# Reciprocal roots of both layer norms moved from VectorE's Newton steps to GpSimd's power

## The chip, the core and the metric

The kernel runs on one core of one Trainium2 chip. The metric is the device time of one execution in microseconds; less is better. The core has five engines that run their own instruction queues and wait for each other by semaphores: TensorE (PE), VectorE (DVE), ScalarE (ACT), GpSimd (POOL) and SyncE (SP), which here only issues DMAs.

## The reference

One transformer layer over x of 8 batches, 256 tokens, 256 features, in fp32. Attention has 32 query heads (two sets of 16) over 16 key and value heads of 16 features, with a causal mask and a full softmax. The MLP is a gated one of 1024 features plus a routed one of 128, scaled by a weight from the two largest of 8 router logits. Both halves end in a norm without weights:

```
m = mean(z); v = var(z)                      # over the 256 features
norm(z) = (z - m) / sqrt(v + 1e-5)
x1  = norm(x + (y1 - sigmoid(x Wlam) * y2) Wo)
out = norm(x1 + shared_mlp(x1) + routed_mlp(x1) * comb)
```

y1 and y2 are the attention outputs of the two sets of heads. Tokens lie on partitions in two tiles (t = 0, 1) of 128, so a norm of one batch needs 2 tiles x 128 reciprocal roots: a [128, 2] operand, one or two elements in each partition.

## The kernel before, in words

Matrix products are done as three TensorE products of high and low parts (`product`, L624 to L628). The high part is a ScalarE copy, the low part a subtraction on VectorE or GpSimd.

The batches go through a software pipeline, `iteration(i)` for i = 0 to 7 on every engine, each with its own order of work written out by hand. Iteration i holds: the scores and softmax of batch i; the first norm, the router and the gate and up products of batch i-1; the down products and the second norm of batch i-2; and the q, k, v projections of batch i+1.

The first half of an iteration is the score stage: 22 units (`s_unit`, L684 and L689) in a ring of three PSUM banks. Unit u can start only when VectorE has taken the row maximum (`row_max`, L998) of unit u-3. Between the units TensorE does projections (behind units 3, 6, 10), down products of batch i-2 (behind 1, 5, 8, 12), the transposes of x1 (behind 11), and the router (behind 15). VectorE puts one small piece of the first norm of batch i-1 behind each of its first seven row maxima: `norm_mean`, `norm_half`, `norm_seed`, three times `norm_newton`, and `ln_shift` (L983). ScalarE applies it in `first_norm` (L503), behind `first_part(i + 1, 1)`.

The second half has 8 groups of two heads. For each, TensorE makes transposed scores (L710, L714), ScalarE takes exponentials (`exps`, L473), GpSimd sets the masked ones to zero (`causal`, L384, two instructions a group), TensorE multiplies by v (`pv_group`, L738) two groups later, and VectorE copies the result out (`evacuate_pv`, L1019). Behind the last group TensorE transposes y (L751): the first half when groups 0 to 6 are copied, the second when group 7 is. Three MLP units of batch i-1 lie between the groups, and GpSimd makes the low parts of h (`h_rests`, L374). The second norm of batch i-2 starts on VectorE behind the copy of group 0, has a Newton step behind those of groups 1, 2, 3, and its end (`second_norm_end`, L1106, two instructions) behind that of group 4.

GpSimd's queue in an iteration: low part of the next batch's x (`split_xt`, L353); low parts of its projections (`rest_part` L359, `third_part` L365), which take turns with ScalarE's parts; sums of batch i-2; masks and `h_rests`.

VectorE's reciprocal root: half of (v + eps), a first guess from the bits of the float (shift, then subtract from a constant), and three Newton steps. Each step waits for the one before it by a semaphore (`settle`).

After the loop comes a tail: the first norm of batch 7, the rest of batch 6's MLP and its second norm, the MLP of batch 7 in 9 units (`gu_units`, `mlp_unit`, `h_rests`), and then `last_tile` for both tiles. There VectorE alone does two sums, the statistics, the root and the normalisation of a tile, and SP stores it.

Of the kernel before, what the change touches and what calls it, by code (L numbers as in the profile page):

```python
# [52 lines left out]
NEWTON = 3  # L53
LN_STEPS = 2 * TT + 3 + (TT + 1) * NEWTON
NORM1_STEPS = LN_STEPS + 1
# [32 lines left out]
RSQRT_SEED = float(0x5F3759DF - 0x400000)  # L88
# [4 lines left out]
I32 = mybir.dt.int32  # L93
# [5 lines left out]
def build_layer(nc, x, xT, w_proj, w_out, w_gu, w_down, w_router, out):  # L99
    with ExitStack() as ctx:  # L100
# [46 lines left out]
        ln_i = sb("ln_i", [P, 2, TT], I32)  # L147
# [60 lines left out]
        attn_step = sem("attn_step")  # L208

# [118 lines left out]
        def _(pool):  # L328
# [9 lines left out]
            pool.wait_ge(const_step, STACKS + 4)  # L338
# [16 lines left out]
            def rest_part(b, n):  # L355
                pool.wait_ge(qk_raw_done, (b - 1) * QK_JOBS + n + 1)
                pool.wait_ge(qk_h_done, b * QK_JOBS + n + 1)
                raw = psum_order(rest_slot(b, n))
                pool.tensor_tensor(raw, raw, part_order(0, n), ALU.subtract).then_inc(qk_rest_done, 1)  # L359

# [37 lines left out]
            def iteration(i, has_next, has_prev, has_last):  # L398
                if has_next:
                    split_xt(i + 1)  # L400
                    for n in range(QK_JOBS):
                        rest_part(i + 1, n)
                        third_part(i + 1, n)
# [8 lines left out]
                for g in range(1, GROUPS):  # L412
                    causal(i, range(g, g + 1))
                    if has_prev and g - 1 in FF_SCORES:
                        n = FF_SCORES[g - 1]
                        h_rests(i - 1, range(n, n + 1))
# [10 lines left out]
            h_rests(B - 1, range(FF_UNITS))  # L427
# [3 lines left out]
        def _(act):  # L431
# [66 lines left out]
            def first_norm(b):  # L498

                act.wait_ge(attn_step, (b + 1) * ATTN_STEPS)  # L500
# [426 lines left out]
        def _(dve):  # L927
# [22 lines left out]
            def norm_half(which, step, settle):  # L950
                settle()
                step(dve.tensor_scalar(ln_t[:, which, 0, :], ln_mv[:, which, :, 1], EPS, 0.5, ALU.add, ALU.mult))

            def norm_seed(which, step, settle):

                seed = ln_i[:, which, :]
                settle()
                step(dve.tensor_scalar(seed, ln_t[:, which, 0, :].bitcast(I32), 1, None, ALU.logical_shift_right))
                settle()
                step(dve.tensor_scalar(ln_t[:, which, 1, :].bitcast(I32), seed, -1.0, RSQRT_SEED, ALU.mult, ALU.add))  # L960

            def norm_newton(which, step, settle):

                half_var, r, a = ln_t[:, which, 0, :], ln_t[:, which, 1, :], ln_t[:, which, 2, :]
                settle()
                for t in range(TT):
                    step(dve.scalar_tensor_tensor(a[:, t:t + 1], r[:, t:t + 1], r[:, t:t + 1], half_var[:, t:t + 1], ALU.mult, ALU.mult))
                settle()
                step(dve.scalar_tensor_tensor(r, a, 1.5, r, ALU.subtract, ALU.mult, reverse0=True))

            def first_norm_step(n, step, settle):

                if n == 0:
                    norm_mean(0, step, settle)
                elif n == 1:
                    norm_half(0, step, settle)
                elif n == 2:
                    norm_seed(0, step, settle)
                elif n < NEWTON + 3:
                    norm_newton(0, step, settle)  # L980
                else:
                    settle()
                    step(dve.scalar_tensor_tensor(ln_shift[:, :], ln_mv[:, 0, :, 0], -1.0, ln_t[:, 0, 1, :], ALU.mult, ALU.mult))  # L983

# [110 lines left out]
            def second_norm_start(b, step, settle):  # L1095
# [3 lines left out]
                norm_half(1, step, settle)  # L1099
                norm_seed(1, step, settle)  # L1100

            def second_norm_end(b, step, settle):
                settle()
# [5 lines left out]
            def last_tile(t, step, settle):  # L1109
# [3 lines left out]
                half_var, r, a = ln_t[:, 1, 0, one], ln_t[:, 1, 1, one], ln_t[:, 1, 2, one]  # L1113
# [10 lines left out]
                settle()  # L1124
                step(dve.tensor_scalar(half_var, ln_mv[:, 1, t, 1:2], EPS, 0.5, ALU.add, ALU.mult))  # L1125
                settle()
                step(dve.tensor_scalar(ln_i[:, 1, one], half_var.bitcast(I32), 1, None, ALU.logical_shift_right))  # L1127
                settle()
                step(dve.tensor_scalar(r.bitcast(I32), ln_i[:, 1, one], -1.0, RSQRT_SEED, ALU.mult, ALU.add))  # L1129
                for _ in range(NEWTON):  # L1130
                    settle()
                    step(dve.scalar_tensor_tensor(a, r, r, half_var, ALU.mult, ALU.mult))  # L1132
                    settle()
                    step(dve.scalar_tensor_tensor(r, a, 1.5, r, ALU.subtract, ALU.mult, reverse0=True))  # L1134
                settle()
                dve.tensor_scalar(z, z, ln_mv[:, 1, t, 0:1], r, ALU.subtract, ALU.mult).then_inc(out_done, 1)  # L1136

            def iteration(i, has_prev, has_last):
# [5 lines left out]
                for u in range(S_UNITS):  # L1144
                    row_max(i, u)
                    if has_prev:

                        if u < NEWTON + 4:
                            first_norm_step(u, *before)
# [13 lines left out]
                for g in range(GROUPS):  # L1163
# [96 lines left out]
```

## Time and profile before

| | |
|---|---|
| median of 3 runs | 504.98 us (504.73 to 506.27) |
| profiled execution: its own time | 506.3 us |
| its span, first to last instruction | 504.6 us |
| TensorE busy | 426.5 us, 85% |
| VectorE busy | 329.9 us, 65% |
| ScalarE busy | 238.7 us, 47% |
| GpSimd busy | 226.6 us, 45% |
| mean granted TensorE clock | 0.947 of 2.4 GHz |

A row of a timeline is an instruction (or several alike, xN): start in us from the span's start, duration, engine, line of the kernel, operation, output<-input by the program's names, shapes. In brackets stands how long the engine had been idle before and what ended that. PE is TensorE's matmuls, PEld its weight loads.

### The profile page before, as it was taken

To read this page: it belongs to the slowest core of one execution; us is meant where nothing else is said; L and a number is where in the kernel's file an instruction comes from. 1 tells how busy PE (TensorE), PEld (TensorE's weight loads), DVE (VectorE), ACT (ScalarE), POOL (GpSimd) and SP (SyncE) were. 2 spreads that over 40 slices of the span, in tenths; PEclk is the share of its full clock that TensorE was granted. 3 is DMA by queue.
4 is the path that set the end of the run, shared out by engine and by line. 5 is a ranking of instruction groups with operands and counts; after the bars stand their busy time and mean duration, and the time that the engine had idled before them with its cause. 6 is when DMAs were issued, how large, how long until landed. Compare 5 with 4: busy or idle time off the path is not lost. (4 is left out here: it accounts for less than half of the span.)

```text
span 504.6 us, 10452 instructions
## 1 busy us (share of the span) xinstructions
PE 426.5 (85%) x4008; PEld 340.2 (67%) x4008; DVE 329.9 (65%) x882; ACT 238.7 (47%) x532; POOL 226.6 (45%) x283
## 2 busy tenths in 40 slices
PE   5106596799999999989899999999999998997994
PEld 5105334676688758976698568865887678766984
DVE  3503614873478586886787677857786769776685
ACT  4600384237535672548434843576255831582240
POOL 8200465426526572447334743656254731373041
PEclk9755979879999999999999999999999999999999
DMA  8793498128703690249212950378024910000000
GB/s 299 165 124 49 117 132 173 32 84 115 99 2 99 92 133 27 68 90 136 58 38 83 126 105 11 107 92 121 22 76 74 136 46 0 5 2 22 1 23 21
DMA packets 34371, 40.43 MB, mean 80 GB/s; under 512 B 3856, under 2 KB 27920, under 8 KB 34064
## 3 DMA queue, kind: packets, MB, share of 16 engines
q1 hardware_dynamic: 34320, 39.75, 43.3%
q8 instruction: 32, 0.52, 0.5%
q14 instruction: 19, 0.16, 0.1%
HBM read 27.94 MB, written 11.53 MB: 78 GB/s over the span
## 5 line engine op out<-in xcount | busy, mean ns | idle before, releaser
L998 DVE TENSOR_REDUCE neg_max<-ring 128x2 f32<-128x512 f32 (+3 forms) x176 | 105.8, 635 | 40.2 <-PE ring L689 38.3
L473 ACT ACTIVATE prob<-ring 128x512 f32<-128x512 f32 x192 | 100.7, 612 | 14.7 <-PE ring L710 14.5
L374 POOL TENSOR_TENSOR h_lo<-h_full,h_hi 128x256 fp32r<-128x256 f32 x72 | 53.0, 736 | 108.0 <-ACT h_hi L433 108.0
L384 POOL TENSOR_SCALAR_AFFINE_SELECT prob<-prob 128x512 f32<-128x512 f32 x128 | 83.9, 679 | 32.7 <-ACT prob L473 32.7
L626 PE MATMUL ff<-x1T_hi,wg_lo 128*128 128x256 f32 x288 | 85.7, 298 | 1.2 <-DVE h_full L1014 1.2
L628 PE MATMUL ff<-x1T_hi,wg_hi 128*128 128x256 f32 x288 | 80.3, 279 | 0.0
L627 PE MATMUL ff<-x1T_lo,wg_hi 128*128 128x256 f32 x288 | 80.3, 279 | 0.0
L684 PE MATMUL ring<-mask_b,ident_b 128*128 128x128 bf16 (+2 forms) x176 | 46.0, 262 | 32.4 <-DMA k_stack<-qk_parts_dram 27.2
L481 ACT ACTIVATE gate_t<-ff 128x256 f32<-128x256 f32 x72 | 27.6, 384 | 76.5 <-PE ff L628 73.7
L689 PE MATMUL ring<-k_stack,q_stack 96*128 96x256 bf16 (+3 forms) x512 | 61.2, 241 | 0.0
L738 PE MATMUL ybank<-prob,v_ones 128*32 128x256 f32 (+1 forms) x1024 | 55.7, 335 | 3.3 <-issue 2.0
L626 PEld LDWEIGHTS ff<-x1T_hi,wg_lo 128*128 128x128 f32 x288 | 54.2, 188 | 4.7 <-DVE h_full L1014 3.2
L627 PEld LDWEIGHTS ff<-x1T_lo,wg_hi 128*128 128x128 f32 x288 | 54.3, 188 | 0.0
L1008 DVE SCALAR_TENSOR_TENSOR gate_t<-gate_t,ff 128x256 f32<-128x256 f32 x72 | 30.1, 418 | 36.7 <-ACT gate_t L481 36.0
L628 PEld LDWEIGHTS ff<-x1T_hi,wg_hi 128*128 128x128 f32 x288 | 54.1, 188 | 0.0
L1019 DVE COPY yv<-ybank 128x256 f32<-128x256 f32 x64 | 27.0, 422 | 40.6 <-PE ybank L738 40.6
L359 POOL TENSOR_TENSOR rest<-rest,parts 128x512 f32<-128x512 f32 x21 | 24.4, 1161 | 64.5 <-ACT parts L433 64.4
L710 PE MATMUL ring<-q_stack,k_stack 98*128 98x512 bf16 x128 | 41.4, 396 | 8.0 <-ACT prob L473 4.2
L738 PEld LDWEIGHTS ybank<-prob,v_ones 128*32 128x32 f32 x1024 | 27.4, 109 | 27.8 <-DVE yv L1019 7.5
L684 PEld LDWEIGHTS ring<-mask_b,ident_b 128*128 128x128 bf16 x176 | 17.4, 99 | 40.6 <-issue 27.4
L433 ACT ACTIVATE rest<-ybank 128x512 f32<-128x512 f32 x21 | 12.5, 594 | 67.6 <-PE ybank L628 67.6
L689 PEld LDWEIGHTS ring<-k_stack,q_stack 96*128 96x128 bf16 x512 | 38.0, 103 | 3.6 <-issue 1.1
(166 smaller groups left out, 954.8 us busy)
## 6 DMA issues: line engine op xcount, KB each, us to landing
q_stack<-qk_parts_dram SPq DMA_DIRECT2D x48, 256.0 KB, 9.5
qk_parts_dram<-parts SPq DMA_DIRECT2D x72, 128.0 KB
k_stack<-qk_parts_dram SPq DMA_DIRECT2D x8, 384.0 KB, 14.8
xt_raw<-xT SPq DMA_DIRECT2D x8, 256.0 KB, 2.8
k_stack<-qk_parts_dram SPq DMA_DIRECT2D x8, 256.0 KB, 11.7
xz<-x SPq DMA_DIRECT2D x8, 256.0 KB, 3.6
out<-xz SPq DMA_DIRECT2D x7, 256.0 KB, 2.2
prob<-w_gu SPq DMA_DIRECT2D x1, 1152.0 KB, 7.0
```

Source lines behind the costliest of these rows:

```text
L374: pool.tensor_tensor(h_lo[:, n, :], h_full[:, n % RING, :], h_hi[:, n, :].bitcast(F32), ALU.subtract).then_inc(h_lo_done, 1)
L384: pool.affine_select(out=v, in_=v, compare_op=ALU.is_ge, fill=0.0, base=0, pattern=[[0, 2], [HALF, 2], [0, 2], [1, HALF]], channel_multipl ...
L473: act.activation(prob[:, g % RING, u, :], ring[u][:, :], ACT.Exp, scale=SCALE).then_inc(exp_done, 1)
L626: pe.matmul(o, lhs_lo, rhs_hi, start=first, stop=False)
L627: pe.matmul(o, lhs_hi, rhs_lo, start=False, stop=False)
L628: return pe.matmul(o, lhs_hi, rhs_hi, start=False, stop=last)
L684: pe.matmul(o[:, :, keys - HALF:keys], ident_b[:, :], mask_b[:, :].unsqueeze(1).to_broadcast([P, len(columns), HALF]), start=True, stop=Fa ...
L689: mm = pe.matmul(o[:, j, :], q_stacks[b % STACKS][rows, row, block, i * P:(i + 1) * P], k_stacks[b % STACKS][rows, row, block, 0:keys], st ...
L710: mm = pe.matmul(ring[u][:, :], keys_of(b, rows, n, slice(0, P)), q_pair(b, rows, n, slice(0, 2 * T)), start=True, stop=True)
L738: mm = pe.matmul(bank[V_COLS * j:V_COLS * (j + 1), t * P:T], v_ones[:, t, 2 * g + j // 2, :], p, start=(t == 0), stop=(t == TT - 1))
L998: dve.tensor_reduce(neg_max[:, columns.start:columns.stop, i], ring[u % RING][:, 0:len(columns) * keys].rearrange("p (h k) -> p h k", k=keys),
L1008: dve.scalar_tensor_tensor(gate_t[:, n % RING, :], gate_t[:, n % RING, :], 1.0, ff[n % 2][:, 0:T], ALU.add, ALU.mult).then_inc(gate_done, 1)
```

## The change

All reciprocal roots leave VectorE. GpSimd computes v + eps with a `tensor_scalar` and raises it to the power -0.5 with a `tensor_tensor` against a constant tile `minus_half`, set once at the start. For the first norm it also makes -mean and the product -mean * root (`ln_shift`). VectorE keeps the statistics (`norm_stats`, `norm_mean`) and the normalisation; ScalarE's `first_norm` waits for the new semaphore `norm1_scale`.

In GpSimd's queue the first norm's scale stands behind `split_xt` and ahead of the first `rest_part`; the second norm's behind the mask of group 3. `second_norm_end` on VectorE now stands behind the copy of group 5, not 4. In the tail `first_scale(7)` comes first, `second_scale(6)` behind the low parts of MLP units 0 and 1, `second_norm_end` behind unit 4 as `SCALE_UNIT + 2`, and the last two tiles' scales behind all of h.

```diff
-NEWTON = 3
-LN_STEPS = 2 * TT + 3 + (TT + 1) * NEWTON
-NORM1_STEPS = LN_STEPS + 1
+LN_STEPS = 2 * TT
+NORM1_STEPS = LN_STEPS
+SCALE_STEPS = 4
+SCALE_GROUP, SCALE_UNIT = 3, 2
+LAST_STEPS = 3
...
+            def first_scale(b):
+                base = b * SCALE_STEPS
+                pool.wait_ge(attn_step, (b + 1) * ATTN_STEPS)
+                if not is_first(b):
+                    pool.wait_ge(x1_done, b * TT)
+                pool.tensor_scalar(ln_t[:, 0, 0, :], ln_mv[:, 0, :, 1], 1.0, EPS, ALU.mult, ALU.add).then_inc(norm1_scale, 1)
+                pool.tensor_scalar(ln_t[:, 0, 2, :], ln_mv[:, 0, :, 0], -1.0, 0.0, ALU.mult, ALU.add).then_inc(norm1_scale, 1)
+                pool.wait_ge(norm1_scale, base + 2)
+                pool.tensor_tensor(ln_t[:, 0, 1, :], ln_t[:, 0, 0, :], minus_half[:, :], ALU.pow).then_inc(norm1_scale, 1)
+                pool.wait_ge(norm1_scale, base + 3)
+                pool.tensor_tensor(ln_shift[:, :], ln_t[:, 0, 2, :], ln_t[:, 0, 1, :], ALU.mult).then_inc(norm1_scale, 1)
+
+            def second_scale(b):
+                pool.wait_ge(norm2_step, (b + 1) * LN_STEPS)
+                if not is_first(b):
+                    pool.wait_ge(out_done, b * TT)
+                pool.tensor_scalar(ln_t[:, 1, 0, :], ln_mv[:, 1, :, 1], 1.0, EPS, ALU.mult, ALU.add).then_inc(norm2_scale, 1)
+                pool.wait_ge(norm2_scale, 2 * b + 1)
+                pool.tensor_tensor(ln_t[:, 1, 1, :], ln_t[:, 1, 0, :], minus_half[:, :], ALU.pow).then_inc(norm2_scale, 1)
...
                     split_xt(i + 1)
+                if has_prev:
+                    first_scale(i - 1)
+                if has_next:
                     for n in range(QK_JOBS):
...
                     causal(i, range(g, g + 1))
+                    if has_last and g == SCALE_GROUP:
+                        second_scale(i - 2)
...
-            h_rests(B - 1, range(FF_UNITS))
+            first_scale(B - 1)
+            h_rests(B - 1, range(SCALE_UNIT))
+            second_scale(B - 2)
+            h_rests(B - 1, range(SCALE_UNIT, FF_UNITS))
+            for t in range(TT):
+                one = slice(t, t + 1)
+                pool.wait_ge(last_norm_step, LAST_STEPS * (t + 1))
+                if t == 0:
+                    pool.wait_ge(out_done, (B - 1) * TT)
+                pool.tensor_scalar(ln_t[:, 1, 0, one], ln_mv[:, 1, t, 1:2], 1.0, EPS, ALU.mult, ALU.add).then_inc(last_scale, 1)
+                pool.wait_ge(last_scale, 2 * t + 1)
+                pool.tensor_tensor(ln_t[:, 1, 1, one], ln_t[:, 1, 0, one], minus_half[:, one], ALU.pow).then_inc(last_scale, 1)
...
-                act.wait_ge(attn_step, (b + 1) * ATTN_STEPS)
+                act.wait_ge(norm1_scale, (b + 1) * SCALE_STEPS)
...
-                        if u < NEWTON + 4:
-                            first_norm_step(u, *before)
+                        if u == 0:
+                            norm_mean(0, *before)
...
-                        elif g <= NEWTON:
-                            norm_newton(1, *norm2)
-                        elif g == NEWTON + 1:
-                            second_norm_end(i - 2, *norm2)
+                        elif g == SCALE_GROUP + 2:
+                            second_norm_end(i - 2)
```

## Rows read from the trace of the kernel before


**Rows 1.** The page's first part: busy us (share of the span) xinstructions

```profile
PE 426.5 (85%) x4008; PEld 340.2 (67%) x4008; DVE 329.9 (65%) x882; ACT 238.7 (47%) x532; POOL 226.6 (45%) x283
```

**Rows 2.** Windows: stretch, its us, busy (instructions) by engine, clock, DMA, GB/s

```profile
309.00:319.00 10.00, 10.00 (x99) 9.74 (x98) 9.58 (x26) 4.53 (x8) 3.48 (x3) 1.00 0.16 46
...
99.80:106.40 6.60, 5.85 (x33) 5.48 (x34) 3.50 (x8) 3.47 (x7) 2.52 (x3) 0.50 0.30 86
465.00:468.40 3.40, 3.40 (x18) 3.40 (x18) 0.82 (x2) 0.00 (x0) 0.02 (x1) 0.52 0.00 0
```

**Rows 3.** Waits, 88 to 110 us: us in total, times, longest

```profile
PE ring L684 <- DVE neg_max L998: 3.1, 4, 1.4
```

**Rows 4.** Timeline, pass 1, VectorE and GpSimd: start, us, instruction, idle before

```profile
94.68 0.69 DVE L998 TENSOR_REDUCE neg_max<-ring 128x4 f32<-128x512 f32 x1 [0.15 <-PE ring L689]
...
95.56 1.17 POOL L359 TENSOR_TENSOR rest<-rest,parts 128x512 f32<-128x512 f32 x1 [4.72 <-ACT parts L433]
...
95.67 1.07 DVE L969 SCALAR_TENSOR_TENSOR ln_t<-ln_t 128x2 f32<-128x2 f32 x1
```

**Rows 5.** Tile ln_t: ns min/median/max of one line

```profile
L969 DVE SCALAR_TENSOR_TENSOR ln_t<-ln_t x45: 160/163/1085, 94.4 to 486.7; 128x2 f32<-128x2 f32 x45
```

**Rows 6.** Timeline, pass 7, TensorE

```profile
422.29 0.23 PE L684 MATMUL ring<-mask_b,ident_b 128*128 128x128 bf16 x1 [0.57 <-DVE neg_max L998]
```

**Rows 7.** Timeline, last MLP, VectorE and TensorE

```profile
481.44 0.67 DVE L952 TENSOR_SCALAR ln_t<-ln_mv 128x2 f32<-128x2 f32 x1
...
482.42 0.41 DVE L1008 SCALAR_TENSOR_TENSOR gate_t<-gate_t,ff 128x256 f32<-128x256 f32 x1
...
483.35 0.39 PE L626 MATMUL ff<-x1T_hi,wg_lo 128*128 128x256 f32 x1 [1.20 <-DVE h_full L1014]
```

**Rows 8.** Timeline, the end, TensorE and VectorE

```profile
497.52 0.28 PE L628 MATMUL ybank<-wd_hi,h_hi 128*128 128x256 f32 x1
...
498.91 0.48 DVE L1119 SCALAR_TENSOR_TENSOR xz<-ybank,comb,xz 128x256 f32<-128x256 f32 x1
...
499.89 0.18 DVE L1123 BATCH_NORM_AGGREGATE ln_mv<-ln_stats 128x2 f32<-128x6 f32 x1
...
502.02 0.41 DVE L1136 TENSOR_SCALAR xz<-xz,ln_mv,ln_t 128x256 f32<-128x256 f32 x1
```

**Rows 9.** GpSimd's instructions by form: busy us, mean ns | idle before

```profile
L374 POOL TENSOR_TENSOR h_lo<-h_full,h_hi 128x256 fp32r<-128x256 f32 x72 | 53.0, 736 | 108.0 <-ACT h_hi L433 108.0
...
L353 POOL TENSOR_TENSOR xt_lo<-xt_raw,xt_hi 128x512 fp32r<-128x512 f32 x7 | 9.0, 1281 | 10.1 <-ACT xt_hi L433 9.5
...
L1255 POOL MEMSET const-float32-1.0<- 128x1 f32 x1 | 0.1, 98 | 0.0
```

**Rows 10.** Timeline, start of the kernel, GpSimd

```profile
9.54 0.29 POOL L340 TENSOR_SCALAR_AFFINE_SELECT ident<-ident 128x128 f32<-128x128 f32 x1 [0.23 <-POOL v_ones L337]
```

**Rows 11.** Timeline, pass 1, TensorE: units 7, 10 and 11

```profile
96.49 0.23 PE L684 MATMUL ring<-mask_b,ident_b 128*128 128x128 bf16 x1
...
100.55 0.29 PE L684 MATMUL ring<-mask_b,ident_b 128*128 128x128 bf16 x1 [0.93 <-DVE neg_max L998]
...
103.57 0.33 PE L684 MATMUL ring<-mask_b,ident_b 128*128 128x128 bf16 x1
```

**Rows 12.** Timeline, pass 5, second half: GpSimd, VectorE, TensorE's loads

```profile
343.85 1.30 POOL L384 TENSOR_SCALAR_AFFINE_SELECT prob<-prob 128x512 f32<-128x512 f32 x2 [1.32 <-ACT prob L473]
...
348.43 1.41 POOL L384 TENSOR_SCALAR_AFFINE_SELECT prob<-prob 128x512 f32<-128x512 f32 x2 [1.32 <-ACT prob L473]
...
348.90 1.08 DVE L1106 TENSOR_SCALAR xz<-xz,ln_mv,ln_t 128x256 f32<-128x256 f32 x2
...
351.87 0.25 PEld L738 LDWEIGHTS ybank<-prob,v_ones 128*32 128x32 f32 x8 [0.18 <-POOL prob L384]
...
352.32 0.42 PEld L751 LDWEIGHTS ybank<-ident,yv 128*128 128x128 f32 x4 [0.20 <-DVE yv L1019]
```

More of the change, by code:

```diff
@@ L87 @@
 EPS = 1e-5
-RSQRT_SEED = float(0x5F3759DF - 0x400000)
 F32 = mybir.dt.float32
@@ L92 @@
 BF16 = mybir.dt.bfloat16
-I32 = mybir.dt.int32
 ALU = mybir.AluOpType
@@ L146, in build_layer @@
         ln_shift = sb("ln_shift", [P, TT])
-        ln_i = sb("ln_i", [P, 2, TT], I32)
+        minus_half = sb("minus_half", [P, TT])
         gate_t = sb("gate_t", [P, RING, T])
@@ L208, in build_layer @@
         attn_step = sem("attn_step")
+        norm1_scale, norm2_scale = sem("norm1_scale"), sem("norm2_scale")
+        last_scale = sem("last_scale")
         gu_full, gate_th_done, gate_done, h_done, h_hi_done, h_lo_done = (sem(n) for n in ("gu_full", "gate_th_done", "gate_done", "h_done", "h_hi_done", "h_lo_done"))
@@ L337, in _ @@
             pool.memset(v_ones[:, :, :, HEAD_DIM:V_COLS], 0.0).then_inc(const_step, 1)
-            pool.wait_ge(const_step, STACKS + 4)
+            pool.memset(minus_half[:, :], -0.5).then_inc(const_step, 1)
+            pool.wait_ge(const_step, STACKS + 5)
             for m in (ident, ident_b):
@@ L948, in norm_mean @@
                     step(dve.bn_aggr(ln_mv[:, which, t, :], ln_stats[:, which, t, :]))
[L950 to L983, printed above, removed]
             def split_xt(b):
@@ L1098, in second_norm_start, with second_norm_end @@
                 norm_mean(1, step, settle)
[L1099 to L1103, printed above, removed]
+            def second_norm_end(b):
+                dve.wait_ge(norm2_scale, 2 * (b + 1))
                 z = xz[b % X_SLOTS]
@@ L1112, in last_tile @@
                 one = slice(t, t + 1)
-                half_var, r, a = ln_t[:, 1, 0, one], ln_t[:, 1, 1, one], ln_t[:, 1, 2, one]
                 dve.wait_ge(last_shared_full, t + 1)
@@ L1123, in last_tile @@
                 step(dve.bn_aggr(ln_mv[:, 1, t, :], ln_stats[:, 1, t, :]))
[L1124 to L1136, printed above, removed]
+                dve.wait_ge(last_scale, 2 * (t + 1))
+                dve.tensor_scalar(z, z, ln_mv[:, 1, t, 0:1], ln_t[:, 1, 1, one], ALU.subtract, ALU.mult).then_inc(out_done, 1)
             def iteration(i, has_prev, has_last):
@@ L1208, in _ @@
             first = stepper(attn_step, B * ATTN_STEPS - NORM1_STEPS + TT)
-            for n in range(NEWTON + 4):
-                first_norm_step(n, *first)
+            norm_mean(0, *first)
             x1T_second(B - 1)
@@ L1222, in _ @@
                     second_norm_start(B - 2, *norm2)
-                if 1 < n < NEWTON + 2:
-                    norm_newton(1, *norm2)
-                if n == NEWTON + 2:
-                    second_norm_end(B - 2, *norm2)
+                if n == SCALE_UNIT + 2:
+                    second_norm_end(B - 2)
             last_step, last_settle = stepper(last_norm_step, 0)
```

## The prediction

> **What bounds the kernel now.** I read the page's engine table, then TensorE's waits pass by pass, then the timeline wherever TensorE stands still. A "pass" i is iteration i of the batch loop: scores of batch i, with the first norm and the MLP of batch i-1 and the second norm of batch i-2. TensorE is busy 85% of the span, VectorE 65% [rows 1]. In a middle pass TensorE has no gap while the first norm is made: from 309 to 319 us it is busy 10.00 of 10 us, and VectorE 9.58 [rows 2]. So most of what VectorE loses there is worth nothing. TensorE does wait for VectorE in four places, and these carry the sum:
>
> a) Pass 1. Between 88 and 110 us TensorE waits 3.1 us for row maxima [rows 3]. There is no MLP of an older batch to fill the score stage, so VectorE's maxima pace it, and the norm's small steps stand between them. Some are long: a Newton step of 2 elements (L969) takes 1.07 us [rows 4] where its median is 0.163 [rows 5], because GpSimd's subtraction, begun 0.11 us before, runs until 96.73 [rows 4]; the same happens behind the next maximum. Afterwards TensorE's granted clock is 0.50 (1.2 of its 2.4 GHz) from 99.8 to 106.4 us; in the stretch before, from 96.4, TensorE was busy only in part, standing in those waits [rows 2, 11].
>
> b) Pass 7, which has no projections of a next batch: one wait of 0.57 us [rows 6].
>
> c) The MLP of the last batch: TensorE waits 1.20 us for h_full, because VectorE first makes half and seed of batch 6's second norm [rows 7].
>
> d) The end. TensorE's last matmul is over at 497.80; VectorE goes on alone, two tiles in turn. From the end of the aggregate (500.07) to the last normalisation (502.02) a tile spends 1.95 us in nine small instructions [rows 8].
>
> **The change, part by part.** GpSimd's price. The trace has no GpSimd power and no small GpSimd arithmetic. Two-input subtractions take 736 ns at 256 elements and 1281 at 512 [rows 9]: a line through both leaves 0.19 us at zero elements, so I give each plain small step 0.2. The power X has one or two elements a partition. Below it is the 0.098 of a one-element memset, above it 1.28, a whole 512-element row [rows 9]; it is by far nearest to the small end, and I take double a plain step, 0.4. A GpSimd instruction that waits for one of its own engine starts 0.23 us after that one's end [rows 10]. Two hops between engines cost 0.13 together.
>
> The last two tiles: 1.95 becomes 0.13 + 0.2 + 0.23 + X = 0.96, so 0.99 less per tile. TensorE allows it: tile 1's second sum can't start before the last matmul's end, 497.80, and a hop; it starts at 498.91 now [rows 8] and would at 497.92. Gain 2.0 us. At X = 0.1 it is 2.3 (TensorE cuts the first tile's share to 1.03), at X = 1.28 it is 0.2.
>
> The last MLP: L952, L958, L960 and their waits fill 481.44 to 482.42 and go; batch 6's power needs only to be ready four units later, and GpSimd has gaps there. The wait of 1.20 falls to 0.2: gain 1.0 (0.8 to 1.1). The first norm of batch 7 lies beside down projections of batch 6: 0.1.
>
> Pass 1: maximum 4 runs 94.68 to 95.37 [rows 4]. Without norm steps maxima 5 and 6 follow at once (until 96.6), and maximum 7 waits only for unit 7, which starts at 96.49 [rows 11] and is through by 96.9, and ends near 97.5. Unit 10 then starts at 97.55, not 100.55 [rows 11], and the projection behind it (2.8 us between units 10 and 11 at the low clock) takes 1.4. Unit 11 moves from 103.57 [rows 11] to 99.4. The three waits give 3.0, the clock 1.2: gain 4.2. Everything behind is in order on TensorE and moves with it. Bounds: 2.8 if the clock still falls a little later; 4.7 if the low stretch disappears wholly. The new chain on GpSimd (two steps, power, product and two waits: 3 x 0.2 + 0.4 + 2 x 0.23 = 1.5 us) can begin behind maximum 1, over 2 us ahead of maximum 4 at 94.68, and so is through before GpSimd's subtraction at 95.56 [rows 4], the first that now stands behind it. Each of those waits for ScalarE's part, and each ScalarE part for it; none is late. ScalarE needs the result only behind its second projection part.
>
> Pass 7: the wait of 0.57 and crumbs of earlier ones: gain 0.7 (0.5 to 0.9).
>
> Passes 2 to 6, score stage: 0, covered by TensorE's full row [rows 2]. Were that cover gone, about 2.5 us a pass (the small steps of one norm) would be worth something.
>
> Passes 2 to 7, second half. GpSimd's two steps and their wait (0.83 us) stand behind the mask of group 3, where it idles 1.32 us for ScalarE's exponentials before group 4 [rows 12]. Behind them are only masks whose data isn't there yet, so nothing is late below 1.3 us, and nothing on TensorE below 2.6: before group 6's mask GpSimd idles another 1.32 [rows 12]. The row normalisations (L1106) move one group on, from behind group 4's copy to behind group 5's. Today they meet group 6's mask: the two masks take 1.41 us, where the others take 1.30 [rows 12], and all of that delays group 7's mask, for whose second half TensorE waits at 351.87 [rows 12]. This 0.11 comes back. In turn they now stand ahead of group 6's copy, and meet group 7's mask. VectorE's rows then get the port only at the end of the mask, 351.8, the copy ends at 352.3 to 352.7, and the transposes that start at 352.32 are 0.1 to 0.4 late; their second half waits for group 7's copy, which isn't late. I take +0.05 a pass, 0.3 in all; bounds -0.7 and +2.
>
> On this meeting of engines the rows show full blocking: L969 ends within 0.02 us of GpSimd's instruction [rows 4]. The Trainium skill, SBUF — State Buffer, section "SBUF: two separate sides", says the same: the pair of ports that VectorE and GpSimd share is taken by one instruction for its whole length, and the other stands. By that rule the moved normalisations cost a mask's remainder a pass, as above; by a view in which both only slow down a little, the 0.3 would be 0.
>
> The Trainium skill, GPSIMD Engine Reference, section "Key points", speaks against the change: elementwise work is about twice as fast on VectorE. VectorE's small steps of 0.15 us would become 0.3 by it, and the tail would give 0.2 less. The rows at hand (0.19 at zero elements) speak for less, and two instructions in place of nine outweigh either.
>
> **Sum.** 4.2 + 0.7 + 1.0 + 0.1 + 2.0 - 0.3 = 7.7 us. The span is 504.6 and the profiled execution's own time 506.3, 1.7 around the span; so 498.6 for such an execution. The median of the runs is 504.98, 1.3 under the profiled one; against it the forecast is 497.3.
>
> **The rivals.**
> 1. The clock doesn't come back in pass 1, or falls a little later: between the transposes and the router job TensorE would now stand about 1.8 us waiting for ScalarE's split of x1, which can cost the level again. For it: it fell once behind such waits [rows 2]. Against it: 1.20 us of waiting in the last MLP [rows 7] lowered nothing. Gain 1.4 less, with 0.1 behind: 498.8.
> 2. The power costs a whole row's 1.28 us: the tail gives 0.2, not 2.0: 499.1. For it: powers may be loops in software; against it: so few elements.
> 3. The moved normalisations are paid in full. A pair takes 1.08 against a mask [rows 12]; at 0.7 us net a pass, six passes lose 4.2 instead of 0.3: 501.2.
> 4. The other side: the power is slow, several us. The idle times before the masks of groups 4 and 6 hide it up to 2.6 - 0.43 = 2.2 us. Above, each of six passes pays X - 2.2 and each last tile X - 1.4. Everything else gives 5.7, so 6(X - 2.2) + 2(X - 1.4) = 5.7 at X = 2.7: from there it is slower. At X = 4: 504.98 - 5.7 + 10.8 + 5.2 = 515.3. Nothing in the trace is that slow for its size (2.7 is 2.1 times the dearest row above), but nothing shows the operation either.
> 5. More gain: at the end of pass 7 TensorE also runs at the low level, 465.0 to 468.4, at 0.52 [rows 2]; half of 3.4 us lost is 1.7. Moved by 5 us against whatever decides it, this may vanish: 495.6.
>
> **How the numbers follow.** Forecast 0.50 (495.9 to 498.6), rival 1 0.16, rival 2 0.10, rival 3 0.08, rival 4 0.07, rival 5 0.09. The predicted time is 497.3. The range takes all but rival 4 and the outer part of 3 and 5: 494.8 to 501.0. A measurement of this kernel tells about 0.3% (1.5 us) from no change. Faster: all but rival 4 and a mix of 1, 2 and 3 together: 0.89; within 0.3%: 0.04; slower: 0.07.
>
> **What the profile after would show.** Pass 1: no TensorE wait for neg_max above 0.5 us, unit 11 near 99.4, clock 1.00 between 99.8 and 103. Last MLP: the 1.20 us wait at most 0.3. Tail: from aggregate to normalisation about 0.9 us, with two GpSimd instructions in it, the power about 0.4. Groups 4 to 7: the masks at the same distance as now, the transposes of y at most 0.4 us later against the last mask. Wrong it would be by a power over 2.2 us, by code fetched at its first use longer than the 2 us ahead of 95.56, or by VectorE's copies held behind the normalisations.

## The result

| | runs | median us | lowest to highest |
|---|---|---|---|
| before | 4 | 504.93 | 504.73 to 506.27 |
| after | 4 | 497.36 | 493.56 to 499.81 |

The ratio is 0.985, 95% interval 0.981 to 0.989: 7.6 us less, against a forecast of 7.7. The forecast time was 497.3. But the changed kernel's own runs lie 6.3 us apart, so the match of one median says little. Two more sets of it, timed beside the experiments below, gave ratios of 0.991 (0.987 to 0.994) and 0.984 (0.980 to 0.987). Over all its 16 runs the median is 497.76 and the mean 497.4; the 66 runs of the kernel before that stood beside the experiments have a median of 504.13 and a mean of 504.0. So the change is worth about 6.5 us, known to 1.2 or so either way, since the 16 runs spread over 8 us.

The profiled execution of the changed kernel took 493.56 us, its span 491.8. The page's first part (answers [rows 1]):

```profile
PE 419.9 (85%) x4008; PEld 335.7 (68%) x4008; DVE 277.8 (56%) x676; ACT 238.3 (48%) x532; POOL 244.5 (50%) x334
```

VectorE lost 206 instructions and 52 us; TensorE's instructions are the same, and of the 6.6 us that it is less busy most are clock: the two low stretches of [rows 2] are absent here.

**GpSimd's price** (answers [rows 9]). Tile minus_half and tile ln_t by line, ns min/median/max:

```profile
L372 POOL TENSOR_TENSOR ln_t<-ln_t,minus_half x8: 694/695/716, 89.0 to 460.9; 128x2 f32<-128x2 f32 x8
L382 POOL TENSOR_TENSOR ln_t<-ln_t,minus_half x7: 698/706/706, 172.4 to 472.8; 128x2 f32<-128x2 f32 x7
L466 POOL TENSOR_TENSOR ln_t<-ln_t,minus_half x2: 548/551/554, 485.6 to 488.7; 128x1 f32<-128x1 f32 x2
```

and by form (busy us, mean ns | idle before):

```profile
L374 POOL TENSOR_TENSOR ln_shift<-ln_t 128x2 f32<-128x2 f32 x8 | 1.6, 197 | 0.6
L369 POOL TENSOR_SCALAR ln_t<-ln_mv 128x2 f32<-128x2 f32 x8 | 1.5, 193 | 20.5 <-DVE ln_mv L987 20.5
```

The power costs 0.55 us at one element a partition and 0.70 at two, more than the 0.4 taken; the plain steps cost 0.19 to 0.20, as estimated.

**Pass 1** (answers [rows 3, 4, 11]). TensorE's waits from 84 to 106 us; then GpSimd's chain for the first norm in the timeline:

```profile
PE ff L665 <- ACT x1T_hi L472: 1.4, 1, 1.4
PE ybank L665 <- issue: 0.7, 1, 0.7
PE ring L723 <- DVE neg_max L1002: 0.6, 3, 0.2
```

```profile
88.50 0.19 POOL L369 TENSOR_SCALAR ln_t<-ln_mv 128x2 f32<-128x2 f32 x1 [2.07 <-DVE ln_mv L987]
88.77 0.19 POOL L370 TENSOR_SCALAR ln_t<-ln_mv 128x2 f32<-128x2 f32 x1
89.05 0.72 POOL L372 TENSOR_TENSOR ln_t<-ln_t,minus_half 128x2 f32<-128x2 f32 x1
89.84 0.20 POOL L374 TENSOR_TENSOR ln_shift<-ln_t 128x2 f32<-128x2 f32 x1
```

The 3.1 us of waiting for row maxima are 0.6, none over 0.2. GpSimd's chain takes 1.54 us (1.5 forecast: the dearer power and the shorter waits cancel). Unit 11 starts 11.56 us behind the pass's first matmul, where 15.57 stood before and 11.4 was forecast. The new wait is the one that rival 1 names: 1.4 us for the split of x1, where it said 1.8.

**The second half of a pass** (pass 5, answers [rows 12]): GpSimd, then VectorE.

```profile
335.04 0.19 POOL L380 TENSOR_SCALAR ln_t<-ln_mv 128x2 f32<-128x2 f32 x1
335.32 0.70 POOL L382 TENSOR_TENSOR ln_t<-ln_t,minus_half 128x2 f32<-128x2 f32 x1
336.27 1.31 POOL L407 TENSOR_SCALAR_AFFINE_SELECT prob<-prob 128x512 f32<-128x512 f32 x2 [0.25 <-ACT prob L512]
...
340.85 1.30 POOL L407 TENSOR_SCALAR_AFFINE_SELECT prob<-prob 128x512 f32<-128x512 f32 x2 [1.29 <-ACT prob L512]
...
342.80 1.30 POOL L407 TENSOR_SCALAR_AFFINE_SELECT prob<-prob 128x512 f32<-128x512 f32 x2
```

```profile
343.71 0.42 DVE L1023 COPY yv<-ybank 128x256 f32<-128x256 f32 x1 [2.33 <-PE ybank L777]
344.05 0.72 DVE L1108 TENSOR_SCALAR xz<-xz,ln_mv,ln_t 128x256 f32<-128x256 f32 x2
344.69 0.84 DVE L1023 COPY yv<-ybank 128x256 f32<-128x256 f32 x2
```

The reader is to see three things. The power fits into the idle time before group 4's mask, which shrinks from 1.32 to 0.25 us. Group 6's mask is back at 1.30 from 1.41. And the normalisations (L1108) now stand between the copies of groups 5 and 6. In this pass they don't meet group 7's mask: it ends at 342.80 + 1.30 = 344.10, they follow the copy ahead of them and take 0.72 us. In 11 of the 15 passes 2 to 6 of the changed kernel's three profiles they do meet it, for one in pass 3 of after_third:

```profile
233.97 1.30 POOL L407 TENSOR_SCALAR_AFFINE_SELECT prob<-prob 128x512 f32<-128x512 f32 x2
234.18 0.42 DVE L1023 COPY yv<-ybank 128x256 f32<-128x256 f32 x1 [1.63 <-PE ybank L777]
234.52 1.21 DVE L1108 TENSOR_SCALAR xz<-xz,ln_mv,ln_t 128x256 f32<-128x256 f32 x2
235.66 0.74 DVE L1023 COPY yv<-ybank 128x256 f32<-128x256 f32 x2
```

The pair takes 1.21 us in place of 0.72 and ends 0.46 behind the mask (235.27), while the copy out of PSUM ran beside it in its usual 0.42. The two copies behind the pair are late, and with them the transposes of y: their first weights load 46.7 to 47.1 us into the pass, where it was 46.4 to 46.5 in the same five passes before. Against the end of group 7's mask that is 0.9 to 1.2 us in place of 0.4 to 0.5, so at least 0.5 later, past the 0.4 that was allowed. The last transposes of the pass are only 0.1 later where TensorE's own idle times are alike.

**The end** (answers [rows 8]): last tile on VectorE and GpSimd.

```profile
488.14 0.18 DVE L1124 BATCH_NORM_AGGREGATE ln_mv<-ln_stats 128x2 f32<-128x6 f32 x1
489.28 0.41 DVE L1126 TENSOR_SCALAR xz<-xz,ln_mv,ln_t 128x256 f32<-128x256 f32 x1 [0.95 <-POOL ln_t L466]
```

```profile
488.41 0.19 POOL L464 TENSOR_SCALAR ln_t<-ln_mv 128x1 f32<-128x1 f32 x1 [2.23 <-DVE ln_mv L1124]
488.69 0.55 POOL L466 TENSOR_TENSOR ln_t<-ln_t,minus_half 128x1 f32<-128x1 f32 x1
```

From aggregate to normalisation it takes 0.95 us where 0.96 was forecast, by two errors that cancel: hop 0.09, step 0.19, the wait for its own engine 0.09 (not 0.23), power 0.55 (not 0.4), hop 0.04.

**By stage.** I cut each trace at the first matmul of the output projection (ybank<-wo_hi), which stands in the same place of TensorE's order in every kernel, and at TensorE's last matmul. "Start" ends at the first cut, just ahead of pass 1's maxima; "behind" is what follows TensorE's last matmul. All values are us; "low" lists the stretches in which windows of 1 us show a granted clock under 0.98, more than 8 us into pass 1 and at the last cut. Each row is one profiled execution.

| kernel | start | pass 1 | passes 2-6, mean | pass 7 | last MLP | behind it | low, pass 1 | low, end |
|---|---|---|---|---|---|---|---|---|
| before | 88.00 | 55.44 | 54.14 | 50.61 | 33.06 | 6.80 | 99-107 | 464-469 |
| before_again | 86.27 | 55.53 | 54.15 | 50.72 | 31.81 | 6.82 | 100-104 | none |
| tail_only | 86.17 | 55.42 | 54.31 | 50.83 | 32.09 | 4.85 | 100-104 | none |
| tail_again | 86.33 | 55.76 | 54.35 | 50.81 | 33.38 | 4.85 | 99-103 | 464-468 |
| second_only | 86.36 | 55.37 | 54.26 | 50.69 | 30.99 | 6.59 | 97-105 | none |
| first_only | 84.48 | 53.54 | 54.18 | 49.98 | 33.11 | 6.61 | 101-108 | 459-463 |
| no_tail | 87.58 | 53.52 | 54.48 | 50.00 | 30.32 | 6.70 | 104-112 | none |
| after | 83.64 | 51.63 | 54.33 | 49.90 | 30.11 | 4.86 | none | none |
| after_again | 88.58 | 53.59 | 54.22 | 49.89 | 31.68 | 4.94 | 105-112 | 463-467 |
| after_third | 84.03 | 51.19 | 54.22 | 49.91 | 31.78 | 4.88 | none | 456-460 |
| group4 | 85.49 | 51.69 | 54.16 | 49.91 | 31.63 | 4.88 | none | 457-462 |
| group4_again | 85.49 | 51.83 | 54.26 | 49.88 | 30.17 | 4.84 | none | none |
| mult | 85.31 | 51.71 | 54.45 | 49.81 | 29.96 | 4.58 | none | none |
| more3 | 86.95 | 53.50 | 54.69 | 50.45 | 32.65 | 4.92 | 103-111 | 465-469 |

Against the profile of before, that of after is 12.8 us shorter: 4.4 of these lie ahead of the first norm, where nothing of weight was changed, 1.3 or so are the low stretch at the end, which comes and goes whatever the kernel. What is left, 7.1, is the change in this pair. The starts of the nine kernels with the first norm on GpSimd average 85.7 us, those of the five without 86.6; with values between 83.6 and 88.6 that difference isn't shown to be the change's.

### The profile page after: what moved, and what is told of

It is laid out like the page before. It is cut to its first block, busy times and chain, and to the rows that moved or that the text cites. A ratio compares the mean times of both kernels' runs of the same rounds, so it can differ in the third digit from the quotient of the medians.

```text
span 491.8 us, 10311 instructions
## 1 busy us (share of the span) xinstructions
PE 419.9 (85%) x4008; PEld 335.7 (68%) x4008; DVE 277.8 (56%) x676; ACT 238.3 (48%) x532; POOL 244.5 (50%) x334
## 4 chain that ended last, share of the span: by engine, by line
PE 70%; DVE 13%; DMA 5%; ACT 5%; issue 4%; SPq 2%; POOL 1%; POOLq 0%; DVEq 0%; ACTq 0%
PE ff L665 10%; PE ff L667 9%; PE ff L666 9%; PE ybank L777 9%; DVE neg_max L1002 7%; PE ring L749 6%; PE ring L728 5%; PE ybank L665 4%; PE ring L753 3%; DMA k_stack<-qk_parts_dram 3%; PE ybank L790 3%; PE ybank L666 3%; PE ybank L667 3%; PE ring L723 2%; ACT prob L512 2%
## 5 line engine op out<-in xcount | busy, mean ns | idle before, releaser
L1002 DVE TENSOR_REDUCE neg_max<-ring 128x2 f32<-128x512 f32 (+3 forms) x176 | 104.2, 636 | 52.6 <-PE ring L728 51.9
L665 PE MATMUL ff<-x1T_hi,wg_lo 128*128 128x256 f32 x288 | 85.7, 298 | 0.1
L728 PE MATMUL ring<-k_stack,q_stack 96*128 96x256 bf16 (+3 forms) x512 | 59.2, 236 | 0.0
L728 PEld LDWEIGHTS ring<-k_stack,q_stack 96*128 96x128 bf16 x512 | 36.8, 101 | 3.4 <-issue 1.1
```

What stands on the lines that cost most here:

```text
L665: pe.matmul(o, lhs_lo, rhs_hi, start=first, stop=False)
L728: mm = pe.matmul(o[:, j, :], q_stacks[b % STACKS][rows, row, block, i * P:(i + 1) * P], k_stacks[b % STACKS][rows, row, block, 0:keys], st ...
L1002: dve.tensor_reduce(neg_max[:, columns.start:columns.stop, i], ring[u % RING][:, 0:len(columns) * keys].rearrange("p (h k) -> p h k", k=keys),
```

## The experiments

Each was timed against runs of the kernel before on the same chip.

**1. The parts one at a time.** Each takes one part of the diff into the kernel before. Its core, for the first norm:

```diff
+                if has_prev:
+                    first_scale(i - 1)
...
-                        if u < NEWTON + 4:
-                            first_norm_step(u, *before)
+                        if u == 0:
+                            norm_mean(0, *before)
```

> The kernel before with only the first norm's scale and shift on GpSimd; the second norm and the last tiles keep VectorE's Newton steps. Parts theory (the time saved is the sum of the removed stalls): pass 1 gives 3 us of stalls and about 1.2 us of clock (wo job to wo job 55.4 becomes 51.6), pass 7 gives 0.2 to 0.7, passes 2 to 6 nothing; in all 4 to 5 us less than before, about 500.3. The last MLP's wait of 1.20 us stays, and so does the tail of 1.95 us a tile. Rival (the stalls are the cause, the clock isn't bound to them): low clock stays somewhere in pass 1, 3 us less. Rival (what the change gained is mostly the start-up and the clock of one run): under 2 us less.

500.34 against 503.47, ratio 0.993 (0.991 to 0.996): 3.1 us. Pass 1 and pass 7 took 53.54 and 49.98 us in its profile. This is the first rival's case, which said 3 us: the low stretch is still in pass 1, and with it the gain there is 1.9 us.

For the second norm:

```diff
+                    if has_last and g == SCALE_GROUP:
+                        second_scale(i - 2)
...
-                        elif g <= NEWTON:
-                            norm_newton(1, *norm2)
-                        elif g == NEWTON + 1:
-                            second_norm_end(i - 2, *norm2)
+                        elif g == SCALE_GROUP + 2:
+                            second_norm_end(i - 2)
```

> The kernel before with only the second norm's root (batches 0 to 6) on GpSimd, normalisations behind group 5. Parts theory: last MLP 1.0 us less, passes 2 to 7 together 0.5 to 1.4 us more because the normalisations meet a later mask (the whole change showed 0.08 to 0.38 us more in each pass 2 to 6), so within 0.5 us of before; pass 1 keeps its waits for row maxima and its low clock (55.4 us). Rival (VectorE's load in passes 2 to 6 matters after all, so fewer small steps there save time): 2 us or more less than before.

503.72 against 503.47, ratio 1.001 (0.999 to 1.003): nothing, as the parts theory has it. Taking the second norm's steps off VectorE in passes 2 to 6 buys no time. The wait of [rows 7] is gone (last MLP 30.99 against 31.81, both without the low stretch), and passes 2 to 6 give 0.5 back.

For the tail:

```diff
-                settle()
-                step(dve.tensor_scalar(half_var, ln_mv[:, 1, t, 1:2], EPS, 0.5, ALU.add, ALU.mult))
...
-                dve.tensor_scalar(z, z, ln_mv[:, 1, t, 0:1], r, ALU.subtract, ALU.mult).then_inc(out_done, 1)
+                dve.wait_ge(last_scale, 2 * (t + 1))
+                dve.tensor_scalar(z, z, ln_mv[:, 1, t, 0:1], ln_t[:, 1, 1, one], ALU.subtract, ALU.mult).then_inc(out_done, 1)
```

> The kernel before with only the last two tiles' root on GpSimd. Parts theory: from aggregate to normalisation 0.95 us a tile in place of 1.95, so 2.0 us less at the end and everything else as before: 503.0. Rival (the first tile's gain is lost, since its second sum waits for TensorE's last matmul anyway): 1.0 us less.

503.57 against 503.47, ratio 1.000 (0.998 to 1.002). Both expectations missed. Yet its profile has the 1.95 us: 4.85 behind the last matmul in place of 6.8. Something else is longer in it.

**2. The whole beside its parts.**

> The changed kernel once more, timed on the same chip as its parts. Parts theory: 7.0 to 7.7 us less than before, equal to the three parts' differences added up within 1 us (about 5 + 0 + 2). Rival (the parts hide one another or the gain rests on a clock phase that only the whole has): the whole differs from the sum of its parts by 2 us or more.

498.57 against 503.47, ratio 0.991 (0.987 to 0.994): 4.9 us. The parts add up to 3.1 - 0.2 - 0.1 = 2.8, so the rival's condition (2 us or more apart) was just met, though each of the four medians is known only to 1 or 2 us. The profile of the whole shows why a single set misleads: it drew the low stretch in pass 1 and that at the end. The stretches behind TensorE's wait for x1, from the projection's cut + 12 us, first in after, then in after_again (us, TensorE, loads, VectorE, ScalarE, GpSimd, clock, DMA):

```profile
95.64:99.64 4.00, 2.45 (x24) 1.87 (x23) 3.25 (x6) 2.72 (x5) 2.44 (x3) 1.00 0.42 117
99.64:103.64 4.00, 3.62 (x33) 2.76 (x31) 3.79 (x10) 0.51 (x2) 1.15 (x1) 1.00 0.56 174
103.64:107.64 4.00, 3.72 (x30) 3.34 (x29) 2.80 (x10) 1.76 (x7) 0.73 (x1) 1.00 0.14 27
```

```profile
100.58:104.58 4.00, 2.48 (x25) 1.94 (x24) 2.86 (x6) 2.50 (x6) 2.84 (x3) 1.00 0.34 95
104.58:108.58 4.00, 4.00 (x26) 2.95 (x26) 3.67 (x7) 0.68 (x2) 1.15 (x1) 0.56 0.53 158
108.58:112.58 4.00, 4.00 (x23) 3.98 (x23) 2.06 (x9) 0.74 (x3) 0.00 (x0) 0.58 0.19 65
```

The same program, the same 2.5 us of work in the first 4 us; then the clock stays at 2.4 GHz in one run and falls to 1.2 in the other. Pass 1 is 1.96 us longer for it (53.59 against 51.63).

**3. Controls.** The kernel before again, and the tail again.

> The kernel before once more, unchanged. It shows how far runs of one kernel lie apart and where. Theory A (two things vary from run to run whatever the kernel: when the first score can start, 38.8 to 42.7 us in the profiles so far, and how many stretches TensorE runs at the low clock in pass 1 and at the end of pass 7): the median is within 0.3% of the other runs of before, and its profile differs from the one shown only in these two places. Theory B (each build has a start-up time of its own): its profile starts its first score near 42.7 us again and the median is off by up to 2 us.

503.69 against 504.22, ratio 0.999 (0.996 to 1.001). Theory A holds: start 86.27 and not 88.00, half the low stretch in pass 1, none at the end. It also shows what the low clock cost before. Its stretch in pass 1 was 4 us long and not 8, and pass 1 was no shorter (55.53). Windows from cut + 12 us:

```profile
98.27:102.27 4.00, 3.17 (x20) 2.85 (x21) 2.56 (x6) 1.61 (x3) 1.84 (x2) 0.72 0.32 94
102.27:106.27 4.00, 3.20 (x26) 2.60 (x23) 2.99 (x6) 2.31 (x4) 1.90 (x2) 0.86 0.31 91
```

TensorE is busy only 3.2 of 4 us: its waits absorb what the low clock costs here.

> The last two tiles' root on GpSimd and nothing else, once more. Its profile showed the tail 1.95 us shorter, yet its median was that of before. Theory A (chance in start-up and clock): this time the median is 1 to 2 us under before. Theory B (the build loses those 2 us elsewhere, for instance at the start or in pass 1): the median is that of before again, and the profile shows pass 1 at 55.4 us and a start that is later than in the other parts' builds.

503.83 against 504.22, ratio 0.999 (0.997 to 1.001). By the median this is theory B. But the loss isn't in the start or in pass 1: passes 2 to 6 are 0.16 to 0.20 us longer each (0.8 to 1.0 in all), the last MLP 0.3. The timeline shows where, 43 to 46 us into a pass, first in pass 5 of before_again, then in pass 6 of tail_again, the same matmuls:

```profile
347.63 0.63 PE L738 MATMUL ybank<-prob,v_ones 128*32 128x256 f32 x7
348.55 1.83 PE L738 MATMUL ybank<-prob,v_ones 128*32 128x256 f32 x33 [0.29 <-issue]
```

```profile
402.74 0.63 PE L773 MATMUL ybank<-prob,v_ones 128*32 128x256 f32 x7
404.21 1.27 PE L773 MATMUL ybank<-prob,v_ones 128*32 128x256 f32 x25 [0.84 <-issue]
```

"issue" is idle time for which the profile shows no releaser. Here it is between 0.16 and 1.04 us in nearly every pass of every kernel, it shifts VectorE's next copy by as much, and about half reaches the pass's end: in the tail's two profiles, passes in which these matmuls start 44.35 us behind the cut take 54.17, those with 44.92 take 54.38 to 54.56. The value differs from pass to pass, from run to run (0.47 to 1.04 in four passes of after, 0.24 to 0.29 in three of after_third, the same program), and perhaps by kernel. Its cause stays open: no experiment here varied it.

**4. The normalisations back behind group 4, and the power's own price.**

```diff
-                        elif g == SCALE_GROUP + 2:
+                        elif g == SCALE_GROUP + 1:
                             second_norm_end(i - 2)
```

> The changed kernel with the second norm's normalisations behind group 4's copy, where they stood before the change, in place of group 5's. Passes 2 to 6 took 54.33 us on average in the changed kernel and 54.14 before. If the moved normalisations are what costs this (they meet group 7's mask), they go back to 54.15 and the whole is 1 us shorter than the changed kernel. If it is GpSimd's two new steps behind group 3's mask, nothing changes. If VectorE now waits for the power ahead of group 4's copy, each pass loses up to 0.5 us.

497.0 against 504.22, ratio 0.986 (0.984 to 0.989): 0.8 us under the changed kernel's pooled median, too little for these runs to tell. The profiles tell more, once passes with a like idle time are compared. Where the matmuls behind it start 44.2 to 44.4 us into the pass, the nine passes of second_only, after, after_again and after_third take 54.16 to 54.30 us (mean 54.24): there the normalisations stand behind group 5. The fourteen of before, before_again, tail_only, tail_again, first_only and group4, with them behind group 4, take 53.92 to 54.17 (54.11); group4's own three take 54.08, and their transposes of y load at 46.3 to 46.4, as before. group4 has GpSimd's two steps in the same place as the changed kernel. So the moved normalisations cost 0.13 us a pass, and the steps on GpSimd nothing that shows.

```diff
-                pool.tensor_tensor(ln_t[:, 1, 1, one], ln_t[:, 1, 0, one], minus_half[:, one], ALU.pow).then_inc(last_scale, 1)
+                pool.tensor_tensor(ln_t[:, 1, 1, one], ln_t[:, 1, 0, one], minus_half[:, one], ALU.mult).then_inc(last_scale, 1)
```

and the same at both norms.

> The changed kernel with a product in place of each power: it leaves the root out and measures what the power costs. By the profile of the changed kernel a power takes 0.55 us at one element and 0.70 at two, a product at two 0.20. In the last two tiles 0.35 us each come off the path, and nothing elsewhere, since the powers of the first and second norms are hidden: 0.7 us less than the changed kernel. If the powers in the second halves of passes 2 to 7 delay the masks after all, 0.2 to 0.5 us a pass more, 2 us and over in all.

497.51 against 504.22, ratio 0.986 (0.982 to 0.989). From the changed kernel's pooled 497.76 this can't be told apart, and it is no 2 us less. This kernel leaves the root out, so it prices the power and computes something else. In its profile the product of one element takes 0.19 us and the last tile waits 0.59 in place of 0.95:

```profile
490.76 0.19 POOL L466 TENSOR_TENSOR ln_t<-ln_t,minus_half 128x1 f32<-128x1 f32 x1
```

```profile
490.99 0.41 DVE L1126 TENSOR_SCALAR xz<-xz,ln_mv,ln_t 128x256 f32<-128x256 f32 x1 [0.59 <-POOL ln_t L466]
```

Behind the last matmul this is 4.58 against 4.86 us. Passes 2 to 6 got no shorter (54.45): the power there is hidden. Batch 7's first norm isn't: the router job behind it starts 8.29 us into the last MLP, against 8.50 in after. The expectation had nothing there.

**5. A third set, the tail undone, a slow power.**

> The changed kernel a third time, beside the three kernels below on one chip. Theory A (the gain is 5.5 to 7.7 us, by whether the low clock falls in pass 1): median 4.9 to 7.5 us under before, and in its profile pass 1 is 51.7 us without a low stretch behind the first norm or 53.6 us with one. Theory B (the first measurement was luck, the true gain is that of the parts, 3.5 us): median about 3.5 us under before.

496.03 against 504.44, ratio 0.984 (0.980 to 0.987): 8.4 us. Pass 1 took 51.19 us, without a low stretch. This is past theory A's 7.5 and far from theory B's 3.5.

In the next, the changed kernel has the lines of L1123 to L1136 of before in its last tiles.

> The changed kernel with VectorE's Newton steps back in the last two tiles: both norms on GpSimd, the tail not. Theory A (the 1.95 us that the profile shows at the end are real in every run): 1.9 us more than the changed kernel. Theory B (the tail's change loses them elsewhere, as its own build's median suggests): the same as the changed kernel within 0.7 us.

499.34, ratio 0.990 (0.987 to 0.993): 1.6 us over the changed kernel's pooled median, near theory A's 1.9, and 3.3 over after_third, the lowest of its three sets. In the two profiles 1.8 us is the tail (6.70 against 4.88), and passes 2 to 6 are 0.26 longer each, 1.3 in all: the unexplained idle time is 0.82 to 0.93 in all five. Theory A.

> The normalisations behind group 4's copy, once more. In the traces passes 2 to 6 are 0.1 to 0.2 us shorter than in the changed kernel. Theory A: 0.5 to 1.2 us under the changed kernel in the median. Theory B (the passes differ only by the idle times of TensorE that no wait explains, 0.2 to 1.0 us ahead of a group of matmuls over the probabilities): the same as the changed kernel.

496.96, ratio 0.985 (0.982 to 0.988), no different from after_third within what these runs can tell. Both sets together: median 496.96 of 11 runs against 497.76 of 16. The medians decide neither theory. The 0.13 us a pass from the profiles is 0.8 us over six passes; passes 2 to 6 took 54.26 us on average in this profile only because three of them have idle times of 0.74 to 0.92.

```diff
+                for n in range(3):
+                    pool.wait_ge(norm2_scale, 5 * b + 1 + n)
+                    pool.tensor_tensor(ln_t[:, 1, 2, :], ln_t[:, 1, 0, :], minus_half[:, :], ALU.pow).then_inc(norm2_scale, 1)
```

> The changed kernel with three more powers, each behind a wait for the one before, ahead of the second norm's: as if that power took 0.70 + 3 x 0.79 = 3.1 us. By the prediction's rival 4 the idle times before the masks of groups 4 and 6 cover 2.2 us, and each of six passes pays the rest: 6 x 0.9 = 5.2 us over the changed kernel, 5 to 6 with the last MLP. If the masks have more room than that, under 2 us over. If nothing covers (the masks pace TensorE), 6 x 2.4 = 14 us over.

501.93, ratio 0.994 (0.991 to 0.996): 4.2 us over the changed kernel's pooled median, 5.9 over after_third. Pass 4 on GpSimd, its three extra powers in one row:

```profile
286.69 2.24 POOL L383 TENSOR_TENSOR ln_t<-ln_t,minus_half 128x2 f32<-128x2 f32 x3
289.01 0.69 POOL L385 TENSOR_TENSOR ln_t<-ln_t,minus_half 128x2 f32<-128x2 f32 x1
289.65 1.31 POOL L410 TENSOR_SCALAR_AFFINE_SELECT prob<-prob 128x512 f32<-128x512 f32 x2
...
291.62 2.55 POOL L410 TENSOR_SCALAR_AFFINE_SELECT prob<-prob 128x512 f32<-128x512 f32 x4
...
294.83 1.34 POOL L410 TENSOR_SCALAR_AFFINE_SELECT prob<-prob 128x512 f32<-128x512 f32 x2
```

The chain is 2.3 us longer. Both idle times before masks are used up (groups 5 and 6 now follow at once, x4), and group 7's mask starts 45.2 us behind the cut in place of 44.5: 0.65 late. So the cover is as forecast, and a little larger: the power could have taken 0.70 + 2.3 - 0.65 = 2.35 us, where 2.2 was said. Of the 0.65 a pass pays 0.4 to 0.55 by the table, where the expectation had 0.9; another 0.9 is in the last MLP (32.65 against 31.7, low stretch in both), where TensorE waits 0.9 us for h_full.

## Why the prediction was right

**Pass 1: 4.2, measured 3.8 and 4.25 where the clock holds, 1.85 where it doesn't.** The mechanism is as described, and where the clock holds the size is too. Up to unit 11 it holds in all nine profiles with the first norm on GpSimd: that unit starts 11.5 to 12.0 us into pass 1, against 15.4 to 16.6 in the five without. The step that was mis-sized is rival 1's "1.4 less". The low stretch fell in 4 of the 9 profiles, behind the very wait of 1.4 us for x1's split that was named as its risk, and then costs 1.7 to 2.4 us; TensorE is busy 4.00 of 4.00 us in it. In the kernel before, 4 us of low clock more or less moved pass 1 by 0.1 us (before_again): the stalls for maxima took up the difference. So the forecast's 1.2 us of clock is a gain that a later low stretch takes back with more. With that stretch pass 1 gives 1.9, below the lower bound of 2.8. Rival 1 came in 4 profiles of 9; its chance of 0.16 was too small.

**Pass 7: 0.7, measured 0.7 to 0.8.** second_only and tail_only keep 50.7 to 50.8, first_only has 49.98: it is the first norm's steps.

**Last MLP: 1.0 + 0.1, measured 1.7** (31.81 in before_again, 30.11 in after, neither with the low stretch at the last cut; 1.3 to 1.4 where before and the changed kernel both have it). The 1.20 us wait is gone; second_only shows 0.8 for it. What was mis-sized is the first norm of batch 7, taken at 0.1 because down projections lie beside it. They run out: in second_only the transposes of x1 come later and take 0.84 us in place of 0.60, as ScalarE's normalisation ahead of them isn't through:

```profile
470.47 0.84 PE L812 MATMUL misc<-ident,xz 128*128 128x128 f32 x4
...
472.77 0.36 PE L657 MATMUL ybank<-x1T_hi,wr_lo 128*128 128x256 f32 x1
```

and in after they don't:

```profile
463.27 0.60 PE L820 MATMUL misc<-ident,xz 128*128 128x128 f32 x4
...
465.33 0.35 PE L665 MATMUL ybank<-x1T_hi,wr_lo 128*128 128x256 f32 x1
```

Counted from the cut, the router job starts at 9.05 in the one and 8.50 in the other: 0.55, not 0.1. With the wait that went, 1.15 us in before_again, this is the 1.7. With the low stretch at that place TensorE is slower and hides most of the norm again: first_only's router job starts 0.15 earlier than before's, and its last MLP (33.11 against 33.06) shows nothing of it.

**The last two tiles: 2.0, measured 1.94.** Right, partly by luck: the power is 0.15 dearer and the wait 0.14 cheaper than taken. Rivals 2 and 4 (1.28 us and over 2.7) are out. That the tail alone gave no time doesn't touch it: the trace of no_tail has the 1.8 us back in place, and the two profiles of the tail alone lose 0.8 to 1.0 us in passes 2 to 6 and 0.3 in the last MLP. That leaves 0.6 to 0.8 us of gain where the medians show -0.1 and 0.4, with 95% intervals of -1.2 to 0.8 and -0.6 to 1.4; the full 1.95 lies outside both. Why those passes are longer in both profiles is not explained.

**Passes 2 to 7: -0.3, measured about -0.6.** Passes 2 to 6 are 0.08 to 0.19 us longer on average. The blocking by group 7's mask is there as described, and so is the mask's 0.11 regained. Among passes in which the matmuls behind the unexplained idle time start 44.2 to 44.35 us behind the cut, six of the changed kernel take 54.16 to 54.28 (mean 54.22) and six of before 53.92 to 54.16 (54.09): 0.13 a pass, where 0.05 was taken. group4 at 54.08 shows that the place of the normalisations is what costs it. Rival 3 (0.7 a pass) is out.

Where VectorE's pair of normalisations of SBUF data met the mask, it took 1.21 us in place of 0.72 and ended 0.46 behind it (pass 3 of after_third), while the copy out of PSUM ran beside the mask in its usual 0.42. The Trainium skill, SBUF — State Buffer, section "SBUF: two separate sides", has the shared pair of ports locked for an instruction's whole length: the trace agrees.

**Elementwise work on GpSimd.** The plain steps take 0.193 us where VectorE's of the same two elements take 0.16 (L983 of second_only's trace, median 0.157). The Trainium skill, GPSIMD Engine Reference, section "Key points", has such work about twice as slow there: at this size no run here shows that factor for plain steps. The power is four times a VectorE step, but replaces eight.

**Rival 5** (1.7 more, the low stretch at the end of pass 7) is neither right nor wrong: the stretch fell in 7 of 14 profiles, with and without the change, and costs 1.2 to 1.7 us. It was in the profile of before and not in that of after, so that the pair overstates the gain.

**Sum.** Without the low stretch in pass 1: 3.8 + 0.7 + 1.7 + 1.9 - 0.6 = 7.5. With it: 5.6. A mix by 4 in 9 gives 6.7; the pooled runs have 6.4 to 6.6. The first median, 0.1 from the forecast, is close partly by luck: the forecast counted on a clock that held in 5 profiles of 9, and three sets of the same kernel gave 7.6, 4.9 and 8.4 us. The medians of the parts add up to only 2.8 to 3.3 us. The profiles by stage close that gap in part (the last MLP, the low stretches, the idle times of TensorE); the rest stays open.

## What to carry to other kernels

A chain of tiny dependent steps on a busy engine costs most where nothing else fills the stage: here the first pass, pass 7, the last MLP and the tail gave all of the gain, and five full passes gave none for their share of the 52 us that VectorE saves. Price a wait and the low clock around it together: with the stall gone, a low stretch can fall into work that is full, where it costs more. And compare stage by stage between cuts that every build has, over several profiles, before a difference of under 1% is put down to an edit: two parts of this change have a right trace and a median that doesn't show it.

## What the runs showed of the hardware

- A GpSimd elementwise power costs 0.55 us at one element a partition and 0.70 at two; an estimate from these two is 0.40 + 0.15 per element. A product or a multiply-add costs 0.19 to 0.20 at either. An instruction that waits for its own engine starts 0.09 us after the other's end here, not the 0.23 seen at the kernel's start [rows 10].
- VectorE's work on SBUF stands while a GpSimd mask runs (a pair of 0.72 us took up to 1.22), and its copy out of PSUM doesn't (0.42 beside the mask as elsewhere).
- The granted clock isn't a function of the program alone: behind the same 1.4 us wait it fell in 4 of 9 profiles and held in 5, and within the changed kernel's own three in 1; at the end of pass 7 it fell in 7 of 14. Runs of one kernel spread by 6 to 8 us. The profiles show two sources of it, these stretches and a start that ends between 83.6 and 88.6 us, where the first matmul of the score stage waits for its DMA until 38.2 to 42.4.
- TensorE idles 0.16 to 1.0 us for nothing the profile shows, in nearly every pass, ahead of the same matmuls; kernels with the same order on TensorE differ by up to 0.3 us a pass in the mean of passes 2 to 6.
